# Gather-and-sum over graph edges: four pieces' table numbers in one loaded word, taken apart in registers

## The reference, cut to what matters

```python
def _gnn_layer(x, row, col, W, b, g, beta):        # first graph layer, applied twice
    neigh = x[col]
    agg = jax.ops.segment_sum(neigh, row, num_segments=n)
    ...
    h = (x + agg / deg) @ W.T + b
# second graph layer, once
gathered = edge_weight[:, None] * node_states[edge_src]
aggregate = jax.ops.segment_sum(gathered, edge_dst, num_segments=n)
```

## Time and profile before

| | us |
|---|---|
| three timed runs | 7270.54, 7271.44, 7273.53 (median 7271.44) |
| profiled execution, first to last instruction (span) | 7265.6 |
| median less span | 5.8 |
| POOL's gathers, first to last start: sum0, sum1, sum2 | 997.5 to 2115.4, 2315.8 to 3432.2, 5649.7 to 6798.9 |
| last add of the sums | 2129.99, 3451.59, 6817.40 |

### The profile page before, as it was taken

One profiled execution on the slowest core, in us unless ns is written; L12 is line 12 of the kernel. 1 busy time (PEld: TensorE's weight loads), 2 busy tenths in 40 slices (PEclk: granted clock), 3 DMA queues, 4 the chain that ended last, 5 costly groups with the idle time before them and its releaser, 6 DMA issues. The chain is left out here.

```text
span 7265.6 us, 61921 instructions
## 1 busy us (share of the span) xinstructions
PE 3646.1 (50%) x13991; PEld 2632.2 (36%) x13992; DVE 2657.8 (37%) x6350; ACT 899.9 (12%) x2400; POOL 3769.2 (52%) x3797
## 2 busy tenths in 40 slices
PE   4112974444544445444431222299992455555729
PEld 1001543333333333333221000178881334333517
DVE  5115864444433444444340000011114455555661
ACT  0000950000003000000230000022221100000322
POOL 4772036666663666666537777700005566666321
PEclk7556987777777777777665555599996678787859
DMA  3000113333321333332011000022214233333250
GB/s 136 1 0 30 21 49 92 92 92 92 91 61 61 90 92 91 92 92 83 21 58 59 4 2 8 4 75 81 83 57 137 88 90 91 90 91 91 70 162 18
DMA packets 290147, 497.59 MB, mean 68 GB/s; under 512 B 99253, under 2 KB 182880, under 8 KB 290048
## 3 DMA queue, kind: packets, MB, share of 16 engines
q0 software_dynamic: 163264, 345.19, 16.7%
q1 hardware_dynamic: 125696, 150.28, 6.3%
q10 hardware_dynamic: 1088, 1.05, 0.1%
HBM read 487.50 MB, written 92.89 MB: 80 GB/s over the span
## 5 line engine op out<-in xcount | busy, mean ns | idle before, releaser
L970 PE MATMUL sum_sums<-sum_got,sum_onehot 128*128 x4992 | 1613.7, 484 | 1690.7 <-DVE acc L1132 1360.6
L902 POOL DMA_INDIRECT sum_got<-xn,edge_row x1568 | 1541.5, 983 | 1138.9 <-issue 451.4
L970 PEld LDWEIGHTS sum_sums<-sum_got,sum_onehot 128*128 128x128 f32 x4992 | 1166.3, 244 | 2121.9 <-issue 1915.4
L1132 DVE TENSOR_TENSOR acc<-acc,sum_sums 128x257 f32 (+1 forms) x2496 | 1052.7, 422 | 1777.8 <-remote 1241.3
L902 POOL DMA_INDIRECT sum_got<-h,edge_row x784 | 754.4, 962 | 453.3 <-issue 228.4
L1270 POOL DMA_INDIRECT table<-rec,addr x784 | 802.8, 1024 | 298.5 <-issue 277.4
L1866 PE MATMUL moe_f_ps_y<-xb,moe_f_hT 128*128 128x256 f32 x1792 | 478.8, 399 | 317.3 <-issue 317.2
L1850 PE MATMUL moe_f_ps_h<-moe_f_xT,xb 128*128 128x256 f32 x1792 | 473.1, 396 | 303.9 <-issue 303.9
L1931 DVE TENSOR_TENSOR moe_f_y<-moe_f_ps_y,moe_b 128x256 f32<-128x256 f32 x112 | 42.4, 420 | 1362.4 <-DMA table<-acc 718.5
L1698 POOL DMA_INDIRECT moe_out_c_got<-moe_out,place_i x98 | 95.0, 970 | 824.5 <-PEq L1656 785.1
L1270 POOL DMA_INDIRECT table<-sort_rec,sort_addr x392 | 400.0, 1020 | 201.8 <-issue 122.9
(11 more groups left out here) (460 smaller groups left out, 3297.0 us busy)
## 6 DMA issues: line engine op xcount, KB each, us to landing
xb<-in_L_ffn_W SPq DMA_DIRECT2D x112, 1024.0 KB
sum_got<-xn,edge_row POOLq DMA_INDIRECT x1568
moe_in<-acc SPq DMA_DIRECT2D x28, 512.0 KB
moe_f_xin<-moe_in SPq DMA_DIRECT2D x56, 256.0 KB
moe_out<-moe_f_y SPq DMA_DIRECT2D x56, 256.0 KB
xn<-xb SPq DMA_DIRECT2D x14, 896.0 KB
table<-rec,addr POOLq DMA_INDIRECT x784
sum_got<-h,edge_row POOLq DMA_INDIRECT x784
```

Source lines behind the costliest of these rows:

```text
L902: pool.indirect_dma_start(got[:, c % SU, 0:D], None, source, bass.IndirectOffsetOnAxis(ap=p.edge_row[:, c:c + 1], axis=0)).then_inc(s_got[ ...
L970: mm = nc.tensor.matmul(sums[k % 2][j], onehot[:, (k % QUARTERS) * HALF + j, :], flat(got[:, bass.ds(where[n % PLAN], 1), :]), start=True, ...
L1132: v.tensor_tensor(a, a, sums[k % 2][j], ALU.add).then_inc(s_added[j], 1)
```

## The change

A new helper takes a field of some bits out of a register: by a mask, or by a shift and a mask.

```diff
@@ tensor, step @@
                     if k % QUARTERS == 0:
-                        turn = flat(plan[:, bass.ds(2 * i + k // QUARTERS, 1), :])
-                        _, where = nc.values_load_multi_w_load_instructions(
-                            turn[:, 0:PLAN], ...
-                        _, need = nc.values_load_multi_w_load_instructions(
-                            turn[:, PLAN:], ...
-                    pe.wait_ge(s_landed, at_least_one(pe, need[k % QUARTERS], CH // EU))
+                        _, words = nc.values_load_multi_w_load_instructions(
+                            plan[:, bass.ds(PER * i + k, QUARTERS)], ...
+                    word = words[k % QUARTERS]
+                    where = [field(pe, word, SLOT_BITS * j, SLOT_BITS, SU - 1) for j in range(HALF)]
+                    need = field(pe, word, HALF * SLOT_BITS, GROUP_BITS, CH // EU)
+                    pe.wait_ge(s_landed, at_least_one(pe, need, CH // EU))
@@ vector, loop @@
-                _, tile_regs = nc.values_load_multi_w_load_instructions(
-                    p.tile_of[0][0:1, bass.ds(PLAN * g, PLAN)], (mybir.EngineType.DVE,),
+                _, words = nc.values_load_multi_w_load_instructions(
+                    into[:, bass.ds(QUARTERS * g, QUARTERS)], (mybir.EngineType.DVE,),
...
                 for k in range(QUARTERS):
+                    tile = [field(dve, words[k], TILE_BITS * j, TILE_BITS, NT - 1) for j in range(HALF)]
                     turn = dve.snap(QUARTERS * g + k + 1)
@@ plans @@
-                v.scalar_tensor_tensor(out=plan[:, :, 0:PLAN], ... op0=ALU.mult, op1=ALU.add).then_inc(s_plan, 1)
...
+                c.link(v.scalar_tensor_tensor(out=slots, in0=row_i, scalar=-float(SU), in1=numbers, op0=ALU.mult, op1=ALU.add))
...
+                for j in reversed(range(HALF - 1)):
+                    c.done(v.scalar_tensor_tensor(out=plan, in0=plan, scalar=float(1 << SLOT_BITS), in1=slot[:, :, j],
+                                                  op0=ALU.mult, op1=ALU.add))
+                    c.done(v.scalar_tensor_tensor(out=into, in0=into, scalar=float(1 << TILE_BITS), in1=tile[:, :, j],
+                                                  op0=ALU.mult, op1=ALU.add))
+                    c.settle()
```

More of the change, by code:

```diff
@@ L766, in sum_over_edges @@
                 s("own_" + x) for x in ("s_put", "s_flip", "s_copied", "s_own", "s_taken", "s_kept"))
-        plan = p.plan[0:1, 0:PIECES // PLAN * (PLAN + QUARTERS)].rearrange("a (g v) -> a g v", v=PLAN + QUARTERS)
+        plan, into = (p.plan[0:1, k * PIECES // HALF:(k + 1) * PIECES // HALF] for k in range(2))
         freed = p.plan[0:1, PIECES // PLAN * (PLAN + QUARTERS):]
@@ L1057, in plans @@
                 c.link(v.tensor_single_scalar(row_i, row_i, 16, ALU.arith_shift_right))
[L1058 to L1066, removed]
+                c.link(v.scalar_tensor_tensor(out=slots, in0=row_i, scalar=-float(SU), in1=numbers, op0=ALU.mult, op1=ALU.add))
+                slot, tile = (row.rearrange("a (g j) -> a g j", j=HALF) for row in (slots, p.tile_of[0][0:1, 0:PIECES]))
@@ L1068, in plans @@
+                c.link(v.tensor_scalar(groups_of, groups_of, 1.0, None, ALU.add))
+                c.link(v.tensor_single_scalar(groups_of, groups_of, HALF * SLOT_BITS, ALU.logical_shift_left))
+                v.tensor_tensor(plan, plan, groups_of, ALU.bitwise_or).then_inc(s_plan, 1)
                 dve.wait_ge(s_high, 1)
@@ L1117, in _ @@
             with dve.Fori(0, PIECES // PLAN) as g:
-                _, tile_regs = nc.values_load_multi_w_load_instructions(
-                    p.tile_of[0][0:1, bass.ds(PLAN * g, PLAN)], (mybir.EngineType.DVE,),
-                    min_val=0, max_val=NT - 1,
-                    skip_runtime_bounds_check_because="the table counts the tiles that ended, and is cut at NT - 1")
+                _, words = nc.values_load_multi_w_load_instructions(
+                    into[:, bass.ds(QUARTERS * g, QUARTERS)], (mybir.EngineType.DVE,),
+                    min_val=0, max_val=(1 << (HALF * TILE_BITS)) - 1,
+                    skip_runtime_bounds_check_because="a word holds HALF tiles, each cut at NT - 1")
                 for k in range(QUARTERS):
+                    tile = [field(dve, words[k], TILE_BITS * j, TILE_BITS, NT - 1) for j in range(HALF)]
                     turn = dve.snap(QUARTERS * g + k + 1)
```

27 lines of the change are left out of this document (19 added, 8 removed).

## The result

The changed kernel takes 7457.87 us (median of 4 runs, 7437.31 to 7469.57) against 7271.39 us of the kernel before beside it (7270.54 to 7273.53): a ratio of 1.0254, 95% interval 1.0238 to 1.0271. It is 186 us slower, far outside the predicted 7248 to 7302. The profiled execution spans 7435.6 us against 7265.6.

The account below looks back on a forecast made before the run. Bound: POOL's gathers, held by PE's late-seen count. Sums 0.3 + 0.3 + 2.6 and tail 0.9 gave +4.1 us on 7265.6, 7269.7; the runs' median 5.8 higher, 7275. Range 7263 to 7289, over all cases 7248 to 7302.

Parts of the forecast that it names:

- The bound: In the three sums: POOL's gathers set the pace, held by PE's product count, seen some 8 us late.
- The step that failed: In the sums: DVE and PE idle ahead of the late count, so their register work there costs nothing.
- The term: PE's fields: if one in a hundred new register instructions took 0.701 us, 33 us of sequencer, 3 us at 10%.
- Rival A: Sums' gathers: pace follows other engines' instructions, +30 us at a quarter record each, 7301; sign: sum0 above 1.44; chance 0.19.
- DVE's own time: DVE between quads: fields expose 0.05 us in sum0 and sum1, 0.2 in sum2 (at most 0.3); 10% reaches the clock.
- the prediction's +4 (bound +18): Whole kernel: all terms together +4.1 us, bounds -8 to +18; the forecast's chance 0.62.
- The tails: After each sum's last gather, DVE's remaining quads: 0.9 us more in sum2, under 0.2 in sum0 and sum1.
- Loads and clears: DVE's load falls from 1.100 to 0.334 us, PE saves 1.107 per block; ACT's last clear grows 0.7 us, costing 0.
- the tables' length: Table building on DVE: three operations become twelve, about 3.7 us, 2.6 more, hidden behind the wait for PE: 0.
- the prediction's second case: Tables in sum0: if they take 4 us more, 0.8 us is left, at most lengthening POOL's first wait.
- Rival B: DVE's block heads: its own issue is on the path, so the shorter load gains 23 us, 7249; chance 0.15.
- rival C: PE's loop: instructions fetched anew in each of 76 passes at 1.1 us, +84 us, 7358; chance 0.03.

Follow-up runs that it names:

- e1: Kernel before with only DVE's tile numbers packed (one load of 4 values per block, fields in registers), PE's loads unchanged: 7369.0 us, ratio 1.0133.
- e4: Kernel before, its loads and tables kept, with as many register instructions added on PE as the change's fields need: 7391.1 us, ratio 1.0167.
- e8: Changed kernel with one gather in place of seven for each group behind the first four: 6038.5 us, ratio 0.8305 to the kernel before.
- e17: Changed kernel with POOL waiting behind each group of seven gathers until it has landed: 7539.3 us, ratio 1.0369 to the kernel before.
- e10: Kernel before with the fields' number of register instructions added on DVE in only two quads of four: 7320.2 us, ratio 1.0020.
- e2: Kernel before with only PE's slots and group counts packed, DVE's load of 16 tile numbers unchanged: 7328.7 us, ratio 1.0077.
- e6: Kernel before with PE's packing alone, the four slots taken apart behind PE's last wait of the quad: 7401.9 us, ratio 1.0181.
- e11: Kernel before with PE's packing alone and four quads in a pass of PE's loop in sum0 and sum1: 7397.6 us, ratio 1.0129.
- e3: Kernel before, its loads and tables kept, with as many register instructions added on DVE as the change's fields need: 7372.9 us, ratio 1.0136.
- e9: Kernel before with DVE's loop unrolled once more, two blocks in a pass: 7305.2 us, ratio 1.0000.
- e16: Kernel before with POOL waiting behind each group of seven gathers until it has landed: 7524.6 us, ratio 1.0353.
- e18: Kernel before with POOL waiting behind every second group of seven gathers until it has landed: 7357.0 us, ratio 1.0053.

## Why the prediction was wrong

**The bound: right.** The gathers' pace sets the sums, POOL is held by SP's `s_free`, PE's count comes late while DVE and PE stand idle. That was the fact to ask about, and I wrote "Why the count comes late no row shows" and went on.

**The step that failed** is the sentence after it: "what they do in registers meanwhile costs nothing". It read the idle time as time with nothing to do. While POOL issues without a pause PE and DVE get through a median of some 90 and 50 records at their own pace, and the kernel before needs just about as many until POOL has to wait. The new ones come on top; after 10 us of gathers about half of PE's are long, at 0.7 us each. They delay PE and DVE, SP frees its groups later, and POOL waits 126 us longer for them. e1 to e4 show that the register instructions do it, e8 and e17 that nearly none is long without POOL's long runs of gathers. The term stood in the upper bound with a size: one in a hundred on PE at 0.701 us, 33 us, 3 of them on the path. It was 1185 of 9402, one in eight, and as many on DVE, for which the prediction had none: 841 and 923 us of long ones, while the sums' gathers became 144 us longer. The longest time of L726 in the earlier trace rows was the hint; SP's row of the same helper, 1398 ns at most, with 42 long ones among its 330, was a plainer one.

**Rival A: the direction was right, the size and the rule not.** By the prediction's own sign, a pace above 1.44 us in sum0, it was A: the pace is 1.484. But A gave each register instruction a fixed price, 7301 at a quarter of a record, and all of them at full weight +120. e10 and e17 show that there is no fixed price: half of them on DVE cost 15 us and all 103, and all are nearly free when POOL pauses.

**DVE's own time: right in sum0, above its bound in sum2.** Quads in the tail of sum0 are 2.77 us apart (2.71 before) and the block's head shows 0.92 us of issue in place of 1.02; in sum2 a quad takes 3.77, 0.33 more than before, where 0.2 was the estimate and 0.3 the bound.

```profile
2167.32 0.42 DVE L1160 TENSOR_TENSOR acc<-acc,sum_sums 128x257 f32 x1 [1.13 <-PE sum_sums L987]
...
2170.09 0.42 DVE L1160 TENSOR_TENSOR acc<-acc,sum_sums 128x257 f32 x1
...
2173.73 0.42 DVE L1160 TENSOR_TENSOR acc<-acc,sum_sums 128x257 f32 x1 [0.92 <-issue]
...
6979.82 0.42 DVE L1160 TENSOR_TENSOR acc<-acc,sum_sums 128x256 f32 x1 [0.24 <-issue]
...
6983.59 0.42 DVE L1160 TENSOR_TENSOR acc<-acc,sum_sums 128x256 f32 x1 [0.24 <-issue]
```

With the late counts gone, 14.7 us remain in e17: what the prediction's +4 (bound +18) was about. The tails were sized too small: from the start of a sum's last gather to the end of its last add it takes 24.4, 16.8 and 29.7 us where it took 15.1, 19.9 and 18.9, 17 us more in all for 0.9 expected, mostly because more adds are left to do then.

**Loads and clears: right; the tables' length not.** DVE's load takes 0.344 us and PE's 0.332 in the median, as the earlier trace rows had it; ACT's clear of sum2 7.702 us against 7.008, 0.7 more; DVE's wait at the head of sum2 fell from 28.3 to 23.9, so the tables take 4.4 us longer and not 2.6, hidden there. The packing is thirteen operations (L1079 to L1093), not twelve, and each of the six with two inputs in its loop (L1086, L1088) takes 0.51 to 0.56 us, not 0.31. In sum0 the 3.2 us of wait are used up and the one-hot tables start 0.9 us later behind the remainder by 28, as the prediction's second case had it.

```profile
DVE acc L1097 <- DMA table<-rec,addr: 23.9, 1, 23.9
...
L974 PEldq TENSOR_LOAD <-plan x156: 3/332/711, 1013.8 to 6966.7; - x156
...
L1145 DVEq TENSOR_LOAD <-plan x156: 2/344/718, 1024.6 to 6974.7; - x156
...
L867 ACT ACTIVATE acc<-eps x6: 587/2729/7702, 1002.0 to 5828.2; 128x1568 f32<-128x1568 f32 x1, 128x2923 f32<-128x2923 f32 x1, 128x8102 f32<-128x8102 f32 x1, 128x3136 f32<-128x3136 f32 x1
```

The prediction put the saving of PE's shorter loads at nothing. e4 less e2 gives 62 us for it, e6 and e11 speak against it, and it stays open.

**Rival B fell** (a faster head changed nothing: e1 and e3 are alike), **and so did rival C**: 35 packets of instructions where there were 33, and e9 and e11.

```profile
q8 instruction: 35, 0.57, 0.0%
```

**What stays open.** What the 50 and 90 are: places for the instructions themselves on their way in, or for an entry that each leaves on its way out, such as its record in the profile; every time here comes with a recorded span, and no run tells the two apart. Whether POOL's issuing or the number of gathers under way is what uses them up. Why one chip doesn't show it. Why e6 and e11 cost more than e2 (130 and 92 us against 59). And whether a shorter pause behind each seven gathers would be enough: 0.5 us each would cost 56 us for a sum less the late counts, which was not tried.

## What to carry to other kernels

Before you call register work on an idle engine free, look at the longest time of such instructions by engine, and ask what else counts instructions there: here about 50 records on DVE and 90 on PE fit between two pauses of the engine that issues indirect DMAs, and late in such a run about half of the register instructions take 0.7 us. An idle time that the profile calls "remote", with every instruction before it long done, is a bound whose cause has to be found first; a change that adds instructions may feed it. And time such a kernel on more than one chip: a quarter of this one's time is not there on another.

## What the runs showed of the hardware that was not expected

- While POOL issues indirect DMAs one behind the other, at 1.25 us each, register, semaphore and branch instructions of PE, DVE and SP come to take 0.69 to 0.72 us in place of 0.03 to 0.07 (332 of PE's 697 such register instructions after 10 us of gathers in the changed kernel's sum0, and SP's 53 of 572 in the kernel before). A pause of POOL of about 2 us behind each seven gathers takes this away (e16, e17). One behind each fourteen leaves SP's long ones, 51 of 571, and the late counts (e18).
- The late counts of finished products, 431 us in sum0 of the kernel before, go with the same pauses (60 quads of 208 seen over 4 us late there, none over 0.05 us in e16). That they are the same thing is likely, not shown.
- The length of a loop's body has no part in it: 49 or 96 instructions in a pass of DVE are equal within 0.1% (e9), and a pass of PE of 102 records in place of 134 has 14% long with the fields (e11).
- Two chips of one kind run the same kernel in 7268 and 5545 us. With pauses behind each seven gathers the sums are alike on both (1211, 1219, 1218 and 1210, 1220, 1212 us), and the stages outside them still are not: 7524.6 against 6168.0.
